# Dividing attention heads on GpSimd and projecting them from padded rows inside the neighbouring phases of a four-layer network

## The reference

```python
# layer 0: 16 heads of 8 channels, no mask; the FFN sends each token to one of 8 experts
p = softmax(q @ k.T / sqrt(8));  o = (p @ v).reshape(b, n, 128);  attn = o @ Wo.T + bo
y = relu(x @ W1[e] + b1[e]) @ W2[e] + b2[e];  ffn = y * route_p
# layer 1: causal mask, a learned bias by distance; 2 of 8 experts for a token, densely computed
p = softmax(q @ k.T / sqrt(8) + rel_bias, causal);  attn = (p @ v) @ W_proj + b_proj
ffn = sum over e of w[n, e] * (relu(x @ W1[e] + b1[e]) @ W2[e] + b2[e])
```

## Time and profile before

| | us |
|---|---|
| median of 3 runs (lowest, highest) | 1102.11 (1099.16, 1103.34) |
| the profiled execution, its own time | 1107.07 |
| its span in the trace | 1105.3 |
| a0, attention of layer 0 | 50 to 434 |
| m0, experts of layer 0 and projection | 435 to 507 |
| a1, attention of layer 1 | 545 to 819 |
| p1, projection of layer 1 | 820 to 839 |
| m1, experts of layer 1 | 840 to 910 |

### The profile page before, as it was taken

How to read it: one execution, slowest core, us unless ns; L and a number is a source line. 1 busy time by engine, 2 the same in 40 slices (tenths; PEclk the granted TensorE clock), 3 DMA queues, 4 the chain that set the end, 5 groups by cost and what they waited for, 6 DMA issues and landing times. The chain is left out here.

```text
span 1105.3 us, 22355 instructions
## 1 busy us (share of the span) xinstructions
PE 927.7 (84%) x8663; PEld 478.2 (43%) x8663; DVE 823.7 (75%) x1674; ACT 622.2 (56%) x1318; POOL 137.1 (12%) x146
## 2 busy tenths in 40 slices
PE   5279999999999998993399999999979987765698
PEld 4112222222222213892245545555447765644468
DVE  6598999999999920555488788777836668798587
ACT  4307888888888854442417677676742326223362
POOL 3005400000000060760000000000000002022122
PEclk9558999999999955996659999999988997888699
DMA  4544623214213031761761343343000000000001
GB/s 133 184 97 87 145 71 98 63 37 99 63 37 99 1 96 39 215 202 57 254 140 28 84 93 91 78 92 92 3 2 6 1 1 1 1 0 1 3 6 34
DMA packets 60538, 78.27 MB, mean 71 GB/s; under 512 B 18696, under 2 KB 44065, under 8 KB 60386
## 3 DMA queue, kind: packets, MB, share of 16 engines
q1 hardware_dynamic: 52482, 52.87, 19.3%
q0 software_dynamic: 6896, 23.07, 7.1%
q10 hardware_dynamic: 1056, 0.91, 0.3%
HBM read 51.37 MB, written 17.90 MB: 63 GB/s over the span
## 5 line engine op out<-in xcount | busy, mean ns | idle before, releaser
L792 DVE TENSOR_REDUCE a_negmax<-a_mbank 128x1 f32<-128x1024 f32 (+4 forms) x640 | 488.1, 817 | 76.4 <-PE a_mbank L624 37.0
L756 ACT ACTIVATE a_probs<-a_ebank 128x512 f32<-128x512 f32 (+3 forms) x896 | 434.6, 555 | 194.8 <-PE a_ebank L645 106.2
L617 PE MATMUL a_mbank<-a_moving,a_still 48*128 48x512 bf16 (+4 forms) x1280 | 262.0, 377 | 37.9 <-DMA a_bias_a<-trow 15.7
L645 PE MATMUL a_ebank<-b_moving,b_still 50*128 50x512 bf16 (+4 forms) x1280 | 270.3, 365 | 20.6 <-ACT a_probs L756 17.7
L668 PE MATMUL a_acc<-a_probs,a_slot_v 128*32 128x512 f32 (+3 forms) x1792 | 230.3, 587 | 1.1 <-ACT a_probs L756 1.1
L645 PEld LDWEIGHTS a_ebank<-b_moving,b_still 58*64 58x64 bf16 (+1 forms) x1280 | 84.2, 101 | 264.5 <-ACT a_probs L756 213.1
L617 PEld LDWEIGHTS a_mbank<-a_moving,a_still 56*64 56x64 bf16 (+1 forms) x1280 | 69.6, 103 | 104.4 <-DVE a_negmax L792 63.5
L654 PE MATMUL a_ebank<-a_bias_b,anti 64*64 64x176 bf16 (+4 forms) x1728 | 85.7, 227 | 0.0
L654 PEld LDWEIGHTS a_ebank<-a_bias_b,anti 64*64 64x64 bf16 x1728 | 68.1, 108 | 8.6 <-issue 0.2
L624 PE MATMUL a_mbank<-a_bias_a,anti 64*64 64x176 bf16 (+3 forms) x576 | 65.4, 239 | 0.0
L668 PEld LDWEIGHTS a_acc<-a_probs,a_slot_v 128*32 128x32 f32 x1792 | 35.8, 109 | 54.0 <-issue 38.0
(11 more groups left out here) (360 smaller groups left out, 1162.0 us busy)
## 6 DMA issues: line engine op xcount, KB each, us to landing
a_slot_v<-vo SPq DMA_DIRECT2D x16, 512.0 KB, 5.4
stack<-s_parts SPq DMA_DIRECT2D x16, 384.0 KB
b_moving<-stack SPq DMA_DIRECT2D x64, 96.0 KB, 3.4
b_still<-stack SPq DMA_DIRECT2D x32, 192.0 KB, 4.3
a_still<-stack SPq DMA_DIRECT2D x62, 96.0 KB, 2.6
a_moving<-stack SPq DMA_DIRECT2D x62, 96.0 KB, 2.5
stack<-s_parts SPq DMA_DIRECT2D x16, 256.0 KB
a_bias_b<-trow SPq DMA_DIRECT2D x32, 66.0 KB, 4.4
```

The costliest lines, as they stand in the source:

```text
L617: last = nc.tensor.matmul(mbank[COLS * c:COLS * (c + 1), bank, lo - left:hi - left], S.a_still[rows, pr, at[c]:at[c] + COLS], S.a_moving[r ...
L645: last = nc.tensor.matmul(ebank[COLS * c:COLS * (c + 1), s % NE, lo:512], S.b_still[rows, buf, pr, at:at + COLS], S.b_moving[rows, buf, h, ...
L756: nc.scalar.activation(probs[:, g % 2, j, lows[g]:512], ebank[:, s % NE, lows[g]:512], ACT.Exp).then_inc(p_full, 1)
L792: nc.vector.tensor_reduce(to[:, at:at + 1], mbank[:, (index - 1) % NM, 0:right - left], AX.X, ALU.max, negate=True).then_inc(m_empty, 1)
```

## The change

- **Padded rows are projected as they are.** The host lays Wo and W_proj out as `heads_out`, 128 padded rows for each quad of heads, zero in the rows that hold no value. A tile of 128 tokens is then four 128x128 float32 products straight from `S.vo`, summed in PSUM, with no transpose (`project_tile`).
- **The division is done on S.vo before that**, by GpSimd, one 128x1024 multiply for each quad (`divide_heads`). Its factors come from four sum rows: a DMA gathers them into a 128x32 tile (`gather_sums`), DVE inverts it (`invert`), a DMA stores it to DRAM, and four DMAs load it back, each inverse row onto the 8 rows of its head (`load_inverses`).
- **In a0 and a1** GpSimd runs this chain for quads 0 to 6. DVE's inversions are written into its row of maxima: for quad 0 while it reduces quad 3 (use 4), quad 1 in quad 4 (use 4), and quads 2 to 5 in quads 4 to 7 (use 18). The 8 tiles of the first sequence are projected in the empty slots of turn 7, one slot each, and DVE adds them to x. The bias add moves from DVE (L1091, L883) to GpSimd. In a0 the scatter of rows moves ahead, to turn 1, and the expert fetches are 8 instead of 6.
- **m0 and m1** finish the last quad through the same chain with the DMAs on SP, and project the 8 tiles of the second sequence: in m0 after `hidden` of blocks 10, 13, 16, 19 and four at the end, in m1 as two times four tiles, after pairs 10 and 13. **p1 is gone.** m0 loses its transposes, reciprocals, multiplies and copies.
- Three tiles of a0 move into space that S.xnT and S.xn leave unused; `wot` has four weights instead of five.

```diff
-AHEAD = 6
+AHEAD = 8
+def project_tile(nc, S, layer, t, out):
+    BQ = HEADS // QUAD
+    for q in range(BQ):
+        last = nc.tensor.matmul(out, S.vo[:, t // BT * BQ + q, t % BT * P:(t % BT + 1) * P],
+                                S.heads_out[:, layer, q, :], start=q == 0, stop=q == BQ - 1)
+    return last
+def gather_sums(eng, S, q, sums):
+    return eng.dma_start(sums[:], S.vo[HD:P:VW, q, :].rearrange("j (k c) -> j k c", c=VW))
+def store_inverses(eng, S, inverse):
+    return eng.dma_start(S.inverse_dram.rearrange("(p c) -> p c", c=VW), inverse[:])
+def load_inverses(eng, S, inverses):
+    return [eng.dma_start(inverses[VW * j:VW * j + HD, :],
+                          bass.AP(S.inverse_dram.tensor, SEQ * j, [[0, HD], [1, SEQ]])) for j in range(QUAD)]
+def divide_heads(nc, S, q, inverses):
+    return nc.gpsimd.tensor_tensor(S.vo[:, q, :], S.vo[:, q, :], inverses[:], ALU.mult)
...
# attention_phase, GpSimd
-                pool.wait_ge(m_full, 2 * USES)
+                pool.wait_ge(masks_ready, 1)
                 pool.dma_start(S.sorted_dram, S.empty_rows).then_inc(rows_cleared, 16)
-                for b in range(AHEAD):
-                    pool.wait_ge(m_full, (2 * b + 6) * USES // 2)
-                    fetch_expert(nc, S, b).then_inc(expert_loaded, 16)
...
+            nc.gpsimd.tensor_tensor(S.x[:], S.x[:], S.b_row[:, layer, :].unsqueeze(1).to_broadcast([P, NT, P]), ALU.add
+                                    ).then_inc(biased, 1)
+            nc.gpsimd.memset(inverses[:], 1.0).then_inc(filled, 1)
+            pool.wait_ge(filled, 1)
+            for q in range(NQUAD - 1):
+                pool.wait_ge(acc_empty, 2 * q + 3)
+                gather_sums(pool, S, q, sums).then_inc(sums_loaded, 16)
+                for b in range(2 * q, min(2 * q + 2, AHEAD) if sort else 0):
+                    fetch_expert(nc, S, b).then_inc(expert_loaded, 16)
+                pool.wait_ge(inverted, q + 1)
+                store_inverses(pool, S, inverse).then_inc(inverse_stored, 16)
+                pool.wait_ge(inverse_stored, 16 * (q + 1))
+                for dma in load_inverses(pool, S, inverses):
+                    dma.then_inc(inverses_loaded, 16)
+                pool.wait_ge(inverses_loaded, 64 * (q + 1))
+                divide_heads(nc, S, q, inverses).then_inc(divided, 1)
+                pool.wait_ge(divided, q + 1)
# TensorE, first_pass
+                    elif n >= tiles_from and (n - tiles_from) % tile_every == 0 and (n - tiles_from) // tile_every < BT:
+                        projected((n - tiles_from) // tile_every)
+                        yield
+            def projected(t):
+                n = tiles_from + t
+                pe.wait_ge(m_empty, NQUAD * USES + max(t + 2, NM + 1))
...
+                pe.wait_ge(divided, BATCH * 2)
+                project_tile(nc, S, layer, t, mbank[:, n % NM, 0:P]).then_inc(m_full, 1)
# VectorE
+            def invert(q):
+                dve.wait_ge(sums_loaded, 16 * (q + 1))
+                nc.vector.reciprocal(inverse[:], sums[:]).then_inc(inverted, 1)
             def quad(q, loaded, earlier):
                 for use, what in enumerate(uses):
+                    if use == LATE + 2 and q in (3, 4):
+                        invert(q - 3)
+                    if use == LATE + 16 and q >= 4:
+                        invert(q - 2)
...
# experts_and_projection, GpSimd
                 if b + AHEAD < NB:
                     fetch_expert(nc, S, b + AHEAD).then_inc(expert_loaded[b % AHEAD], 16)
+                if b == 5:
+                    pool.wait_ge(inverses_loaded, 64)
+                    divide_heads(nc, S, NQUAD - 1, inverses).then_inc(divided, 1)
# moe_phase, TensorE
                 output(i)
+                if i in PROJECT:
+                    project(PROJECT.index(i))
# the network
-            project_phase(nc, S, "p1", S.wp1[:], S.b_row[:, 1, :])
```

More of the change, by code:

```diff
@@ L428, in attention_phase @@
     NE = 3
+    layer = 1 if causal else 0
+    tiles_from = NQUAD * USES + (2 if sort else 1)
+    tile_every = (starts[0] - (tiles_from - NQUAD * USES)) // BT
     A_DMA, B_DMA = (96, 176) if causal else (64, 112)
@@ L920, in fetch_expert @@
+            dve.wait_ge(biased, 1)
+            for t in range(BT):
+                if t == 3:
+                    invert(NQUAD - 2)
+                n = tiles_from + t
+                dve.wait_ge(m_full, n + 1)
+                nc.vector.tensor_tensor(S.x[:, t, :], mbank[:, n % NM, 0:P], S.x[:, t, :], ALU.add).then_inc(m_empty, 1)
+            dve.wait_ge(m_empty, NM + NQUAD * USES + 1 + BT)
 def fetch_expert(nc, S, b):
@@ L1039, in _ @@
                     relu(b + 1)
[L1040 to L1046 removed]
+            act.wait_ge(h_done, NB)
         @block.vector
@@ L1089, in _ @@
                     take(b + 2)
-                if b == AFTER - 1:
-                    nc.vector.tensor_tensor(xb[:], S.x[:], bias.unsqueeze(1).to_broadcast([P, NT, P]),
-                                            ALU.add).then_inc(biased, 1)
-                    dve.wait_ge(biased, 1)
-                if b >= AFTER:
-                    project(b - AFTER)
+                if b in BETWEEN:
+                    project(BETWEEN.index(b))
                 result(b)
-            dve.wait_ge(added, NT)
+            for i in range(CT, BT):
+                project(i)
+            dve.wait_ge(added, BT)
             for i in range(4):
@@ L1145, in moe_phase @@
         hid = sb("hid", [P, 2, CH])
+        sums, inverse = (sb(n, [P, VW]) for n in ("sums", "inverse"))
+        inverses = sb("inverses", [P, SEQ])
         gp = ctx.enter_context(nc.psum_tensor(f"{name}_gp", [P, 512], F32))
@@ L1188, in second_bias, with project @@
                 last.then_inc(b_full, 1)
+            def project(k):
+                if k:
+                    pe.wait_ge(projected, k)
+                else:
+                    pe.wait_ge(divided, 1)
+                for t in range(CT):
+                    last = project_tile(nc, S, 1, BT + CT * k + t, pr[:, t * P:(t + 1) * P])
+                last.then_inc(product, 1)
             hidden(0)
@@ L1209, in _ @@
                                      ).then_inc(h_done, 1)
+        @block.gpsimd
+        def _(pool):
+            pool.wait_ge(inverses_loaded, 64)
+            divide_heads(nc, S, NQUAD - 1, inverses).then_inc(divided, 1)
+            pool.wait_ge(divided, 1)
         @block.sync
         def _(sp):
+            gather_sums(sp, S, NQUAD - 1, sums).then_inc(sums_loaded, 16)
+            sp.wait_ge(inverted, 1)
+            store_inverses(sp, S, inverse).then_inc(inverse_stored, 16)
+            sp.wait_ge(inverse_stored, 16)
+            sp.wait_ge(filled, 1)
+            for dma in load_inverses(sp, S, inverses):
+                dma.then_inc(inverses_loaded, 16)
             sp.wait_ge(wT_ready, 1)
@@ L1254, in _ @@
                     last.then_inc(added, 1)
+                if i in PROJECT:
+                    k = PROJECT.index(i)
+                    part = S.x[:, BT + CT * k:BT + CT * (k + 1), :]
+                    dve.wait_ge(product, k + 1)
+                    nc.vector.tensor_tensor(part, part, pr[:].rearrange("p (t c) -> p t c", c=P), ALU.add
+                                            ).then_inc(projected, 1)
                 if e == E - 1:
@@ L1449, in project_y @@
                 for i in range(G):
-                    last = nc.tensor.matmul(po[:, g % 2, tile(i)], yT[:, g % 2, i, :], S.wot[:, 4, :],
+                    last = nc.tensor.matmul(po[:, g % 2, tile(i)], yT[:, g % 2, i, :], S.wot[:, 3, :],
                                             start=True, stop=True)
```

220 lines of the change are left out of this document (68 added, 152 removed).

## The result

| | before | after |
|---|---|---|
| median of 4 runs each | 1100.63 us | 1122.59 us |
| ratio, 95% interval | | 1.0198 (1.0157 to 1.0239) |
| span of the profiled execution | 1105.3 | 1122.5 |

A forecast was written before the change was run, and what follows sets the result against it. It took DVE to bound a0, PE a0's tail (at 1.2 GHz), a1 and m1, and GpSimd's queue m0. Terms 2 - 7 - 4.6 + 2 + 0.5 + 4.5 - 19.7 + 7.1 = -15.2 us gave a 1087 us median, range 1075 to 1101.

The forecast's parts named there:

- Term 1: In a0, six added 128x32 reciprocals on DVE, the limiting engine, cost +2 us (0 to 2.3).
- Term 2: In a0's tail, dense tiles bring PE's clock back to full: -7 us (-5.4 to -10.7); moved scatters lie on GpSimd alone.
- Term 3: In m0, GpSimd's queue limits, with fewer spread-fetch pairs, one division, then single spreads 1.54 us apart: -4.6 us (0 to -7).
- Term 4: In a1, the gather-to-divide chain takes 9.9 to 13.8 us; DVE waits in quad 4: +2 us (0 to +5.2); reciprocals +0.5.
- Term 5: In a1's tail, eight tiles in groups with 0.48 us of idle time cost +4.5 us (3.1 to 7.1).
- Term 6: Phase p1 disappears as a whole: -19.7 us.
- Term 7: In m1, eight tiles on a PE that is 97% busy cost +7.1 us.
- Rival B: Each of 14 GpSimd divisions blocks DVE 2.12 us through the shared port in a0 and a1: 1116.7 us, slower; chance 0.04.
- Rival A: The clock stays at 1.2 GHz in a0's tail, +12.3 us in place of -7: 1106 us; chance 0.10.

The follow-up runs named there:

- run 1: Changed kernel with the 1.5 MB clearing of the sorted rows issued as late as in the kernel before; span 1123.4 us.
- run 5: Kernel before with only the clearing of the sorted rows issued early, right behind the mask; 1135.1 us, where the kernel before takes 1130.35 on that chip.
- run 2: Changed kernel with a0's gathers and expert fetches for quads 2 to 5 moved to the middle of a turn; span 1103.0 us.
- run 6: Kernel before with its six expert fetches issued two by two when SP loads the next turn; 1146.3 us, 16 more than the kernel before there.
- run 10: Changed kernel with 6 experts fetched in a0 instead of 8; 1124.2 us.
- run 11: Changed kernel with one of four products in each tile of a0's tail; the tail took 13.1 us less than before, no total given.
- run 3: Changed kernel with a1's inversions of quads 2 to 5 at use 30 instead of 18; span 1108.3 us.
- run 8: Run 7's kernel with a1's tail tiles one group later and m1's division held until DVE has the expert weights; ratio 0.9929 to the kernel before.
- run 4: Changed kernel with GpSimd's divisions cut to 32 of 1024 columns, all DMAs and waits kept; span 1117.4 us.
- run 7: Changed kernel with late clearing, gathers of quads 2 to 5 and all fetches mid-turn in a0, a1's inversions at use 30; ratio 0.9951 to the kernel before.
- 14 to 17: Two measurements each of mid_early and of mid_early with the clearing ahead of the late loads; the latter's ratios 0.9894 and 0.9968 to the kernel before.
- before_early_clear: The kernel of run 5: kernel before with the clearing of the sorted rows issued right behind the mask; 1135.1 us.
- mid_early: Run 2's kernel plus run 8's layer 1 edits, early clearing and scatters kept; ratios 0.9952 and, measured again as mid_early_b, 0.993 to the kernel before.

## Why the prediction was wrong

- **The step that failed** is that the sum has no term for the transfers that GpSimd issues in a0. The sentence under 2 that the scatters that go ahead "lie on GpSimd alone" says nothing of the clearing ahead of them; the fetches, 8 in place of 6 and tied to the copies, and the gathers were put at nothing without a reason. I had looked at GpSimd as an engine and a queue, not at the DMA engines behind it. I had written in 4 that a chain could be late, but for the transfers of a0 I named no cover and no price. The measured term is +21.5 us in place of +2, 19.5 of the 32.4 us between the forecast and these two executions: three waits of PE of 1.9 to 5.0 us, each with a stretch at 1.2 GHz behind it, 19.1 us in all. The first goes with the clearing (runs 1 and 5), the second with two fetches and a gather (runs 2, 6 and 10), the third with a gather alone (runs 2 and 10). The scatters themselves cost nothing on this kind of chip (run 1). How a gather of 16 KB can cost so much stays open. The mean DMA share of 0.30 in a0 hid that in the kernel before it is 0.78 to 0.85 for 10 us at a turn (253 to 263 and 295 to 305 us):

```profile
253.00:263.00 10.00, 9.46 (x65) 2.53 (x62) 9.10 (x9) 8.78 (x18) 0.94 (x1) 1.00 0.85 179
295.00:305.00 10.00, 9.39 (x63) 2.32 (x59) 9.26 (x8) 8.72 (x18) 0.93 (x1) 1.00 0.78 184
```

- **Term 1**, the inversions in a0: the copies fall behind by 0.2 to 0.3 us in five of the six places where one stands, 1.1 us in all, between the bounds of 0 and 2.3.
- **Term 2**, the tail: -5.9, within its bounds, in part by luck. I had the clock low from the start and raised by the tiles; it was full until 415 us, dipped and returned, and with a quarter of each tile it never fell (run 11). That tiles raise it is not shown, and a reason for its fall was not found. The 5.5 us for a group with a tile at half clock should have been 5.24 by my own sum.
- **Term 3**, m0: -3.7 against -4.6, the mechanism as described. None of the rows shown gives the 1.54 us for a gap between single spreads (those of the kernel before are 2.07 in the mean); they measured 1.64.
- **Term 4**, the chain in a1: the place and the wait were right, the size wrong: the chain takes 15.6 us, not 9.9 to 13.8, and the wait takes the clock with it: +7.8, above the bound of 5.2 (run 3).
- **Term 5**, the tail of a1: +8.2 above the bound of 7.1; a wait for the split of the maxima and a dip of the clock were not in it; one group later the tail costs 5.6 (run 8).
- **Term 6**: -19.6, right. **Term 7**: tiles 7.5 us against 7.1, and 3.5 us that were not in it: products at the lower clock, 1.6 (gate) and 0.9 (output), and 0.9 of the lock.
- **Rival B** ended on the right side by luck, for a wrong reason: the divisions' lock was seen once, in m1, and not in a0 or a1 (run 4). **Rival A** did not come. A rival on SP's loads was missing.

## What to carry to other kernels

Before a transfer is moved, look at what the DMA engines do in the few microseconds in which it will be issued, not at their mean share, and at who waits for the transfers it meets; two queues whose waits end at nearly the same moment in each turn meet in each turn. Where TensorE is the engine that waits, look for a stretch at half clock behind the wait and count it too; in a0 it came to 2.5 to 3.2 us in about half of the cases. A chain of small transfers should be costed by its landings in company: the same four loads kept GpSimd waiting for 1.9 us in a0 and 5.8 in a1.

## What was not expected of the hardware

- The traces of all runs have 31 waits of PE for a DMA of 1.7 to 9.9 us behind the first copy of a0. By the copies, 16 of them cost 2.5 to 3.2 us more than they lasted, with a stretch at 0.50 behind them; 14 cost between 0.5 us less and 2.0 more, and the longest 3.9 more.
- A gather of 16 KB, issued among SP's loads, goes with a wait of PE of 1.5 to 2.3 us, and moved away from them with none (run 2, turn 5).
- On the chips of runs 5 to 8 and 14 to 17 PE and ACT stand still together beside GpSimd's 16 scatters, with no event that the profile shows. In *before_early_clear*, in the tail of a0:

```profile
414.63 0.60 PE L645 MATMUL a_ebank<-b_moving,b_still 50*128 50x512 bf16 x1 [13.18 <-issue]
```

ACT waited 13.0 us in the same stretch, with the same releaser. In *mid_early*, where the scatters stand in turn 1, waits of that kind add up to 8 us there. The stall moves with the scatters: it stands in the tail in run 5, in turn 4 in run 6 and in turn 1 in runs 7, 8 and 14 to 17. On the chips of the other runs no wait of PE of that kind above 1.5 us was found in a0. The kernel before takes 1130 us on the first kind and 1100 on the second; the profile names no cause, and none was tried. That PE waits for instructions there, as the expectation of *mid_early_b* has it, is not shown.
